# A two-layer graph network on one core: another way through the first layer's node stage

## The reference

```python
# layer 0: graph convolution with symmetric normalisation
deg   = segment_sum(w_all, dst_all)              # edges and self loops
norm  = deg**-0.5[src_all] * w_all * deg**-0.5[dst_all]
out   = segment_sum((x @ W)[src_all] * norm[:, None], dst_all)
x     = layernorm(x + relu(out + b))
# layer 1: edges gather node rows, multiply them with a filter of the
# edge's features, sum them per node, two small products on each node
x     = layernorm(x + layer1(x, ...))
```

## Time and profile before

| what | value |
|---|---|
| median of 3 runs | 1307.92 us (1307.69 to 1310.2) |
| the profiled execution's own time | 1308.25 us |
| its span, first to last instruction | 1306.4 us |
| node stage of layer 0, first operation on a tile to the end of the last normalisation | 429.7 to 742.1 us |
| busy over the whole span: TensorE, VectorE, ScalarE, GpSimd | 82%, 64%, 48%, 50% |

### The profile page before, as it was taken

The page is one execution under the profiler, slowest core; times in us unless marked ns, Lnnn a source line. Parts: engine busy times, 40 slices in busy tenths (PEclk is TensorE's granted clock), DMA queues, the critical chain, the costliest instruction groups (busy, mean ns, idle before and its releaser), DMA issues.

```text
span 1306.4 us, 23341 instructions
## 1 busy us (share of the span) xinstructions
PE 1077.2 (82%) x4848; PEld 779.9 (60%) x4848; DVE 840.5 (64%) x2558; ACT 625.2 (48%) x1452; POOL 648.6 (50%) x812
## 2 busy tenths in 40 slices
PE   7389999999997799999999488998998998934443
PEld 7345555555554688888888366666666666623332
DVE  8565554455552588888888456566566566539887
ACT  0233333333332466666666434444444444338887
POOL 0245565565555477777777645555555555310000
PEclk9998888888889799999999889999999999965555
DMA  9959899898899577777777568888788887569998
GB/s 366 413 157 234 219 223 239 243 225 223 224 220 225 184 256 267 257 263 263 261 264 258 202 174 171 169 183 171 168 184 168 169 183 169 90 161 328 349 346 294
DMA packets 179808, 299.39 MB, mean 229 GB/s; under 512 B 18194, under 2 KB 75430, under 8 KB 179766
## 3 DMA queue, kind: packets, MB, share of 16 engines
q1 hardware_dynamic: 126742, 186.72, 42.7%
q0 software_dynamic: 35840, 83.91, 33.3%
q10 hardware_dynamic: 17184, 28.32, 5.7%
HBM read 149.98 MB, written 148.90 MB: 229 GB/s over the span
## 4 chain that ended last, share of the span: by engine, by line
PE 50%; issue 17%; POOL 10%; ACT 6%; DMA 5%; DVE 5%; ACTq 4%; POOLq 2%; SPq 1%; DVEq 0%
PE bank L998 14%; PE bank L987 7%; PE bank L1061 5%; PE bank L1072 4%; PE bank L1082 3%; POOL tiny L474 3%; ACTq L520 3%; DMA node_mem<-sum 3%; PE bank L1070 3%; PE bank L1084 3%; PE bank L1085 3%; POOL tiny L477 3%; PE bank L1054 2%; PE bank L976 2%; POOL z_lo L487 1%
## 5 line engine op out<-in xcount | busy, mean ns | idle before, releaser
L511 POOL DMA_INDIRECT sum<-R_mem,l_sidx x80 | 127.8, 1597 | 173.6 <-ACT R_mem L627 169.5
L460 POOL DMA_INDIRECT sum<-R_mem,sidx_all x80 | 129.8, 1622 | 124.3 <-ACT R_mem L563 113.8
L998 PE MATMUL bank<-G_mem,edge_mem 128*128 128x512 f32 x400 | 189.8, 623 | 0.0
L775 DVE TENSOR_SCALAR node_mem<-bank,bf_c 128x256 f32<-128x256 f32 x80 | 35.0, 478 | 160.8 <-PE bank L987 160.7
L998 PEld LDWEIGHTS bank<-G_mem,edge_mem 128*128 128x128 f32 x400 | 82.8, 207 | 87.4 <-issue 83.6
L1034 PE MATMUL bank<-W0h,zT_hi 128*128 128x512 f32 x320 | 133.2, 416 | 0.7 <-ACT zT_lo L594 0.6
L563 ACT COPY R_mem<-bank 128x512 f32<-128x512 f32 x80 | 46.9, 587 | 170.5 <-PE bank L998 169.7
L1034 PE MATMUL bank<-W0l,zT_hi 128*128 128x512 f32 x320 | 126.1, 394 | 0.0
L1034 PE MATMUL bank<-W0h,zT_lo 128*128 128x512 f32 x320 | 126.0, 394 | 0.0
L487 POOL TENSOR_TENSOR z_lo<-node_mem,z_hi 128x512 fp32r<-128x512 f32 x80 | 104.6, 1308 | 19.4 <-ACT z_hi L600 19.4
L882 DVE SCALAR_TENSOR_TENSOR edge_mem<-edge_mem,Y,bank 128x128 f32<-128x128 f32 x240 | 73.1, 388 | 57.3 <-ACT edge_mem L621 57.3
(11 more groups left out here) (160 smaller groups left out, 2642.6 us busy)
## 6 DMA issues: line engine op xcount, KB each, us to landing
sum<-zeros ACTq DMA_DIRECT2D x42, 512.0 KB, 11.7
filt_d<-node_mem SPq DMA_DIRECT2D x40, 512.0 KB, 6.7
node_mem<-sum SPq DMA_DIRECT2D x80, 256.0 KB, 2.7
G_mem<-x SPq DMA_DIRECT2D x80, 256.0 KB, 2.8
x_d<-node_mem SPq DMA_DIRECT2D x80, 256.0 KB, 2.1
node_mem<-filt_d SPq DMA_DIRECT2D x80, 256.0 KB, 3.7
sum<-node_mem SPq DMA_DIRECT2D x80, 192.0 KB, 2.0
out<-G_mem SPq DMA_DIRECT2D x20, 512.0 KB, 4.2
```

The source lines that it names most:

```text
L460: pool.indirect_dma_start(sum0, bass.IndirectOffsetOnAxis(ap=sidx[:, t:t + 1], axis=0), R[t % 8][:, :], None, compute_op=ALU.add).then_inc ...
L511: pool.indirect_dma_start(sum1, bass.IndirectOffsetOnAxis(ap=l1_sidx[:, t:t + 1], axis=0), R3[t % 8][:, :], None, compute_op=ALU.add).then ...
L998: ins = pe.matmul(bank[j][:, :], M[c][q][:, j * P:(j + 1) * P], G[4 * c + q][:, :], start=(q == 3), stop=(q == j))
```

## The change

In `nodes0` only (and two buffers' shapes):

- z is transposed as it is (four transposes with a plain float identity instead of eight products). The split into hi and lo is made on the way out of PSUM: ScalarE copies the bank to `zT_hi`, VectorE subtracts it from the bank into `zT_lo`. `z_hi`, `z_lo`, `ident_r` and ScalarE's and GpSimd's work on them are gone. Four transpose banks, four `zT` buffers.
- TensorE first does the eight products with `zT_hi`, then waits for `zT_lo` and does the other four.
- relu and residual are taken apart: ScalarE does the relu in place, GpSimd adds `xl`.
- The root is taken for two tiles at once, in every odd step: one Ln, one Exp, seven GpSimd operations on two columns.
- `res` is a ring of 8 and SyncE stores the result of tile s-11.

The core of the diff:

```diff
         def nodes0(s, u):            # SyncE
             if live(s, 0):
-                held(sp_, n_hi, s - 3)
-                held(sp_, n_lo, s - 3)
+                held(sp_, n_tr, s - 3)
                 sp_.dma_start(sl[a], rows(sum0, s))
-                held(sp_, n_res, K_RES * (s - 7))
+                held(sp_, n_sum, s - 7)
                 sp_.dma_start(xl[u], rows(x, s))
-            if live(s, 8):
+            if live(s, 11):
                 held(sp_, n_x1, t + 1)
                 ... two stores of res[a]
         def nodes0(s, u):            # GpSimd
-            if live(s, 6):   five operations on tiny of tile s-6
-            if live(s, 0):
-                pool.wait_ge(n_hi, s + 1)
-                pool.tensor_tensor(z_lo[u], sl[u], z_hi[u], subtract)
+            if live(s, 6) and u % 2:
+                held(pool, n_mv, t + 2)          # t = s - 7, tiles t and t + 1
+                var + EPS; mean * -1
+                held(pool, n_rs, 2 * (g + 1))
+                w3 = w2*w2; settle; w4 = w3*w0; held; w3 = 1.5 - 0.5*w4
+                settle; w5 = w3*w2; settle; w6 = w7*w5
+            if live(s, 4):
+                t, a = s - 4, (u - 4) % 8
+                pool.wait_ge(n_rel, t + 1)
+                pool.tensor_tensor(res[a], res[a], xl[a], ALU.add).then_inc(n_sum, 1)
         def nodes0(s, u):            # ScalarE, in this order
+            if tail: wait n_mv; Ln of two columns
+            if live(s, 2): wait n_tr, n_mm; zT_hi = bank
+            if tail: Exp of two columns
+            if live(s, 4):
+                act.wait_ge(n_pre, t4 + 1)
+                act.activation(res[c], res[c], ACT.Relu).then_inc(n_rel, 1)
+            if live(s, 8): wait n_rstd; normalise res[c]
         def nodes0(s, u):            # VectorE, in this order
             if live(s, 0): wait n_sl, n_xl; sl = xl * dis + sl
+            if live(s, 5):
+                dve.wait_ge(n_sum, t + 1)        # t = s - 5
+                dve.bn_stats(stat[c], res[a]).then_inc(n_bn, 1)
+            if live(s, 2):
+                dve.wait_ge(n_hi, t + 1)         # t = s - 2
+                wait(dve, n_mm, t - 3)
+                dve.tensor_tensor(zT_lo[b], bank[b], zT_hi[b], ALU.subtract).then_inc(n_lo, 1)
+            if live(s, 5): held n_bn; bn_aggr
+            if live(s, 4):
+                dve.wait_ge(n_mm, t + 1)         # t = s - 4
+                wait(dve, n_st[a], 32 * turn(t, a, 8))
+                dve.scalar_tensor_tensor(res[a], bank[4 + c], dis, b0_s, mult, add).then_inc(n_pre, 1)
         def nodes0(s, u):            # TensorE
+            if live(s, 1): wait n_z, n_lo; 4 x pe.transpose(bank[a], sl[a], ident)
+            if live(s, 3): wait n_hi, n_pre; 8 products zT_hi * (W0h, W0l)
+                           wait n_lo;        4 products zT_lo * W0h
```

More of the change, by code:

```diff
@@ L114, in build @@
         eps_c = sb("eps_c", [P, 1])
-        ident_r = sb("ident_r", [P, P], F32R)
         before = sb("before", [P, Q])
@@ L190, in build @@
         junk1 = [b[:, 3 * D:3 * D + 256] for b in node_mem]
-        sl, res, W0_s = ([b[:, q * D:(q + 1) * D] for b in node_mem] for q in range(3))
+        sl, W0_s = ([b[:, q * D:(q + 1) * D] for b in node_mem] for q in (0, 2))
+        res = [b[:, q * D:(q + 1) * D] for q in (1, 2) for b in node_mem]
         xl = G
-        z_hi, z_lo = (ring(name, 4, [P, D], F32R) for name in ("z_hi", "z_lo"))
-        zT_hi, zT_lo = (ring(name, 2, [P, D], F32R) for name in ("zT_hi", "zT_lo"))
+        zT_hi, zT_lo = (ring(name, 4, [P, D], F32R) for name in ("zT_hi", "zT_lo"))
         stat = ring("stat", 4, [P, 6])
-        mv = ring("mv", 4, [P, 2])
-        tiny = ring("tiny", 4, [P, 8])
+        mv = ring("mv", 4, [P, 2, 2])
+        tiny = ring("tiny", 4, [P, 8, 2])
         wst = [b[:, 0:1024].rearrange("p (v d) -> p v d", v=2) for b in node_mem]
@@ L259, in build @@
         n_tr = sem("n_tr")
-        n_zT = sem("n_zT")
         n_mm = sem("n_mm")
-        n_res = sem("n_res")
+        n_pre = sem("n_pre")
+        n_rel = sem("n_rel")
+        n_sum = sem("n_sum")
+        n_bn = sem("n_bn")
+        n_mv = sem("n_mv")
         n_rs = sem("n_rs")
@@ L265, in build @@
         n_x1 = sem("n_x1")
-        n_st = [sem(f"n_st{i}") for i in range(4)]
+        n_st = [sem(f"n_st{i}") for i in range(8)]
         f_trow = [sem(f"f_trow{i}") for i in range(4)]
@@ L319, in build @@
         K_IDX = 3
-        K_RES, K_ROOT = 4, 5
+        K_ROOT = 7
         K_SOFT, K_PROJ, K_PROD, K_MSG = 4, 2, 3, 3
@@ L388, in nodes0 @@
                     sp_.dma_start(sum1[bass.ds(t * P, P), C:D], res[a][:, C:D]).then_inc(n_st[a], 16)
-            skewed(sp_, nodes0, 8, 8, unroll=8)
-            sp_.wait_ge(n_hi, T)
-            sp_.wait_ge(n_lo, T)
+            skewed(sp_, nodes0, 11, 16, unroll=8)
+            sp_.wait_ge(n_tr, T)
             for s in range(T):
@@ L468, in nodes0 @@
             def nodes0(s, u):
[L469 to L474, removed]
+                if live(s, 6) and u % 2:
+                    t, a = s - 7, (u - 7) // 2 % 4
+                    g = t // 2 if isinstance(t, int) else (t - (u - 7) % 8) // 2 + a
+                    w, mean, var = tiny[a], mv[a][:, :, 0], mv[a][:, :, 1]
+                    st = Stage(n_rstd, g, K_ROOT)
+                    held(pool, n_mv, t + 2)
+                    st.mark(pool.tensor_scalar(w[:, 0, :], var, EPS, None, ALU.add))
+                    st.mark(pool.tensor_scalar(w[:, 7, :], mean, -1.0, None, ALU.mult))
+                    held(pool, n_rs, 2 * (g + 1))
+                    st.mark(pool.tensor_tensor(w[:, 3, :], w[:, 2, :], w[:, 2, :], ALU.mult))
+                    st.settle(pool)
+                    st.mark(pool.tensor_tensor(w[:, 4, :], w[:, 3, :], w[:, 0, :], ALU.mult))
@@ L475, in nodes0 @@
                     held(pool, n_rstd, st.reached())
[L476 to L479, removed]
+                    st.mark(pool.tensor_scalar(w[:, 3, :], w[:, 4, :], -0.5, 1.5, ALU.mult, ALU.add))
                     st.settle(pool)
-                    st.mark(pool.tensor_tensor(w[:, 5:6], w[:, 4:5], w[:, 2:3], ALU.mult))
@@ L482, in nodes0 @@
-                    held(pool, n_rstd, st.reached())
-                    st.mark(pool.tensor_scalar(w[:, 6:7], mean, w[:, 5:6], -1.0, ALU.mult, ALU.mult))
-                if live(s, 0):
-                    pool.wait_ge(n_hi, s + 1)
[L486 to L493, removed]
+                    st.mark(pool.tensor_tensor(w[:, 5, :], w[:, 3, :], w[:, 2, :], ALU.mult))
@@ L494, in _ @@
+                    st.settle(pool)
+                    st.mark(pool.tensor_tensor(w[:, 6, :], w[:, 7, :], w[:, 5, :], ALU.mult))
+                if live(s, 4):
+                    t, a = s - 4, (u - 4) % 8
+                    pool.wait_ge(n_rel, t + 1)
+                    pool.tensor_tensor(res[a], res[a], xl[a], ALU.add).then_inc(n_sum, 1)
+            skewed(pool, nodes0, 8, 16, unroll=8)
+            for u in range(8):
+                held(pool, n_st[u], 32 * (T // 8))
             held(pool, s_zero1, 16 * (T4 + 4))
@@ L580, in nodes0 @@
             def nodes0(s, u):
[L581 to L584, removed]
-                if live(s, 2):
[L586 to L604, removed]
+                tail = live(s, 6) and u % 2
+                if tail:
+                    t, a = s - 7, (u - 7) // 2 % 4
+                    g = t // 2 if isinstance(t, int) else (t - (u - 7) % 8) // 2 + a
+                    act.wait_ge(n_mv, t + 2)
+                    act.activation(tiny[a][:, 1, :], mv[a][:, :, 1], ACT.Ln, bias=eps_c[:, :]).then_inc(n_rs, 1)
@@ new lines, in nodes0 @@
+                if live(s, 2):
+                    t2, b = s - 2, (u - 2) % 4
+                    act.wait_ge(n_tr, t2 + 1)
+                    wait(act, n_mm, t2 - 3)
+                    act.copy(zT_hi[b][:, :], bank[b][:, :]).then_inc(n_hi, 1)
+                if tail:
+                    act.wait_ge(n_rs, 2 * g + 1)
+                    act.activation(tiny[a][:, 2, :], tiny[a][:, 1, :], ACT.Exp, scale=-0.5).then_inc(n_rs, 1)
+                if live(s, 4):
+                    t4, c = s - 4, (u - 4) % 8
+                    act.wait_ge(n_pre, t4 + 1)
+                    act.activation(res[c], res[c], ACT.Relu).then_inc(n_rel, 1)
@@ L605, in nodes0 @@
+                if live(s, 8):
+                    t8, c = s - 8, u % 8
+                    k, b = c % 2, c // 2
+                    g8 = t8 // 2 if isinstance(t8, int) else (t8 - c) // 2 + b
+                    act.wait_ge(n_rstd, K_ROOT * (g8 + 1))
+                    act.activation(res[c], res[c], ACT.Identity, bias=tiny[b][:, 6, k:k + 1], scale=tiny[b][:, 5, k:k + 1]) \
                        .then_inc(n_x1, 1)
-            skewed(act, nodes0, 6, 8, unroll=8)
+            skewed(act, nodes0, 8, 16, unroll=8)
@@ L697, in _ @@
             dve.tensor_scalar(part_i[:, 3, :], src_i[:, :], 7, None, ALU.logical_shift_right)
-            dve.tensor_scalar(ident_r[:, :], ident_i[:, :], 0.0, None, ALU.is_equal)
```

(50 more changed lines are left out.)

4 lines of the change are left out of this document (2 added, 2 removed).

## The result

The changed kernel takes 1334.92 us (median of 4 runs, 1334.16 to 1335.63) against 1308.6 us before: a ratio of 1.020, 95% interval 1.0182 to 1.0217. It is slower by 26.3 us, where 35 were forecast, and inside the range of 1324 to 1374.

The account below looks back on a forecast made before the run. The prediction took TensorE to bound the kernel before (3.742 us a tile) and a loop of waits the changed one: 4.13 + 0.05 = 4.18 us, 79 x 0.44 = 35 us more, about 1343 us, range 1324 to 1374.

Parts of the forecast that it names:

- The loop: Node stage: `pre`, ScalarE's relu, GpSimd's addition, `bn_stats`, `zT_lo`, aggregate, next `pre` run in series, 4.13 us a tile.
- Its terms: `pre` 0.75, relu 0.625, addition 1.28, hand-overs 0.03, 0.08, 0.05, then `bn_stats` 0.61, `zT_lo` 0.60, aggregate 0.10 us.
- The largest unknown: GpSimd's root in odd steps, about 2.8 us, just fits before the next addition; if held up, 0.35 us a tile.
- the 0.05: Microseconds a tile added to the loop's 4.13 for GpSimd's root, giving 4.18.
- rival C: GpSimd's root delays the addition or collides with z: 0.2 to 0.35 us more a tile, say 1362 us; 17%.
- rival B: TensorE's clock falls at intervals of some 20 us, 6 us each time, in the node stage: 1375 us; 8%.
- Rival A: The loop doesn't bind the node stage, TensorE still does at 3.31 us a tile: 1274 us, faster; 7%.
- Start and end: Node stage: start some 1.5 us sooner, end 1.8 us later; net 0.3, taken as nothing.
- The port: VectorE and GpSimd: z beside relu misses the addition and gets short; held up by 0.3 us, not the whole operation.

Follow-up runs that it names:

- e3: The changed kernel with GpSimd's addition done twice, the first time into an unused part of node_mem: 1435.58 us, ratio 1.0976 to the kernel before.
- e1: The changed kernel with VectorE's `pre` (product out of PSUM) moved ahead of `bn_stats` and the aggregate, behind z and `zT_lo`: 1314.69 us, ratio 1.0055.
- e5: The changed kernel with `pre` (product out of PSUM) moved from the end of VectorE's step to its head, ahead of z: 1268.29 us, ratio 0.970.
- e7: The changed kernel with SyncE's stores eight steps behind its loads instead of eleven: 1693.42 us, ratio 1.294.

## Why the prediction was right

**The loop.** Right in mechanism, place and sign. The forecast wait in front of `bn_stats`, 1.4 us, is 1.40 in the timeline; e3 lengthens the loop by just what it adds, e1 and e5 open it.

**Its terms.** 4.13 us plus 0.05 for the root were forecast and 4.06 measured. `pre` took 0.72 instead of 0.75, the relu 0.635 (forecast 0.625), the addition 1.275 (1.28), the hand-overs 0.03, 0.08 and 0.03 (0.16 in all, 0.14 measured), `bn_stats` to `pre` 1.28 (1.31). The 0.12 us too much, times 79, is 9.6 us: all of the difference between 35 and 25. Some 0.07 of it lie in these terms, 0.05 in the root. (The prediction's 2.04 us for relu, addition and hand-overs is 2.07 by its own terms; nothing hangs on it.)

**The root of two tiles.** The largest unknown, and mis-sized: scaled from five operations I had 2.8 us. It runs from 557.73 to 559.62 in the changed kernel, 1.9 us, and GpSimd then stands idle 0.81 us before the addition. Scaling by the number of operations was the mistake. In the old root of the last tile 0.8 of the 2.0 us are gaps between its operations, and two of the five take 0.34 and 0.26 us; in the new one the gaps are 0.5 us in all and every operation takes 0.19 to 0.22. The programs differ in the same way: the old root has four `held` between its operations, each with a counter to raise, the new one two, and one of its added operations waits for nothing. So neither the 0.05 nor rival C happened; the distances of `pre` in odd and even steps are alike (4.06 and 4.07).

**TensorE.** 86% busy; forecast some 80%. (The forecast divides distances between starts, the table counts durations, which go on after the last start: 3.20 of 4.06 would be 79%.) The transposes cost 0.35 us for four in e5 (560.09 to 560.44), not 0.45, and TensorE's floor is 3.20, not 3.31. The clock stayed at 1.00 (rival B did not happen; its intervals of 20 us and stretches of 6 us were assumed, from no row). By the Trainium skill (TensorE: Matmul & The Clock Gate, the part on PE-mode transpose) transposes don't count as work for the clock; the trace neither confirms nor refutes it, since the granted clock was 1.00 through the whole stage.

**Rival A.** TensorE did not bind, because the loop did. Its price was nearly right all the same: 1274 was given, and with the loop opened it is 1268.

**Start and end.** The end is 1.8 us longer, as forecast. The 1.5 us at the start did come, but two things hid them. From the first z to the first product it is 5.11 us (430.87 to 435.98) against 6.66 (429.74 to 436.40), so 1.55 sooner. From there to the first `pre` it is 4.87 us against 4.39: the products run 0.43 us apart until the clock rises and 0.23 after, and more of them fall before the rise (the granted clock from 438 to 440 us is 0.52 against 0.67). And the stage's first z comes 1.13 us later than before, since the first loads are issued 1.06 us later; why, no run shows. So both ends together cost 1.9 us, where 0.3 was forecast.

**The port.** The prediction said that z is held up in part when it meets a GpSimd operation, and saw no cost since they don't meet. That holds for the changed kernel (z 0.74). The expectation of e1 forgot that its new order makes them meet, and was 33 us off. "In part" was a misreading of the earlier trace rows. There z ends at 558.97, 0.55 us after `z_lo` (558.42), and so it is in all 72 tiles of the kernel before in which z starts during `z_lo`, 0.6 to 1.1 us after it; in e1 it is the same 0.55 in all 74 tiles in which z starts 0.1 to 0.9 us after the addition. So z always does its last 0.55 us after GpSimd has ended, and what it loses is only a matter of when it starts: 0.3 us in the earlier trace rows, 0.8 in e1. The Trainium skill (SBUF — State Buffer, the section on its doors and the shared port pair) says that the one that starts first holds the pair for its whole instruction and the other is blocked fully. The traces agree. The kernel before paid for this too, 0.3 us a tile, under TensorE's time.

## What to carry to other kernels

When work is taken off a busy engine and its result must come back to it, count how many of the engine's own steps lie between the hand-off and the wait in program order: with only one short operation between them, the path through the other engines is in series with everything behind the wait, and no engine's busy share tells of it. The cure is the order, not the engine: `pre` at the head of the step turned 1335 us into 1268 with the same instructions. After each reordering look again at which VectorE operation with both tensors in SBUF now meets GpSimd, and at what stands behind a waiting store in a DMA queue.

## What the runs showed of the hardware

- z, 512 columns with both tensors in SBUF, takes 0.74 us alone, 1.03 on average in the kernel before, where it starts during `z_lo`, and 1.56 (mean of 65) when it starts just behind GpSimd's addition. Each time it ends 0.55 us after GpSimd's operation. The operations with one side in PSUM and `bn_stats` did not get longer beside one: in e5 `pre` takes 0.75 us, `zT_lo` 0.67 and `bn_stats` 0.69, beside the addition as without it.
- It goes the other way round too. In e5 an operation of the root on two columns, 0.19 to 0.22 us elsewhere, starts just behind z and ends 0.05 us after it:

```profile
561.07 0.74 DVE L832 SCALAR_TENSOR_TENSOR node_mem<-G_mem,dis,node_mem 128x512 f32<-128x512 f32 x1
561.13 0.73 POOL L479 TENSOR_TENSOR tiny<-tiny 128x2 f32<-128x2 f32 x1 [0.37 <-ACT tiny L598]
```

- Four transposes of a plain float tile take 0.35 us in a dense stream. The eight products that they replace took 0.89.
- In e7 TensorE is busy 60% of the time, and in each of the turns between 555 and 605 us the clock falls to the lower level:

```profile
560.00:562.00 2.00, 0.06 (x1) 0.00 (x0) 0.00 (x0) 0.00 (x0) 0.00 (x0) 1.00 0.84 269
562.00:564.00 2.00, 0.40 (x2) 0.40 (x3) 1.28 (x3) 0.00 (x0) 0.00 (x0) 0.62 0.02 6
564.00:566.00 2.00, 2.00 (x8) 1.71 (x7) 1.39 (x4) 0.57 (x2) 0.00 (x0) 0.50 0.00 0
...
568.00:570.00 2.00, 1.64 (x5) 0.92 (x3) 0.00 (x0) 0.00 (x0) 0.95 (x6) 0.68 0.81 258
570.00:572.00 2.00, 0.00 (x0) 0.00 (x0) 0.00 (x0) 0.00 (x0) 0.00 (x0) 1.00 0.63 214
```

The columns are those of the earlier trace rows. The products run at half clock, and the clock comes back as they end. The chain through SyncE hides it there. In the changed kernel, idle 14% in pieces of 0.4 and 0.7 us, it never fell inside the stage.
